# Expert results summed per token in DRAM by accumulating transfers, with tiles of 256 and 128 rows in turn

## The reference

```python
global_idx, weights = _route(tokens, ...)              # two of 8 experts per token, softmax of two scores
h = gelu(einsum('nd,edh->enh', tokens, W1) + b1[:, None, :])      # 256 -> 1024
out_all = einsum('enh,ehd->end', h, W2) + b2[:, None, :]          # 1024 -> 256
out = sum(weights[..., None] * out_all[global_idx, arange(N)[:, None]], axis=1)
x = x + gb * out                                       # gb: one vector per batch
```

## Time and profile before

| what | us |
|---|---|
| median of 3 runs | 3407.97 (3407.96 to 3409.85) |
| the profiled execution's own time, its span | 3422.0 |
| TensorE busy in it | 2651.8 |
| VectorE, ScalarE, GpSimd busy | 1756.1, 1196.3, 565.7 |

### The profile page before, as it was taken

The page is one execution under the profiler, slowest core; times in us unless marked ns, Lnnn a source line. Parts: engine busy times, 40 slices in busy tenths (PEclk is TensorE's granted clock), DMA queues, the critical chain, the costliest instruction groups (busy, mean ns, idle before and its releaser), DMA issues.

```text
span 3422.0 us, 77336 instructions
## 1 busy us (share of the span) xinstructions
PE 2651.8 (77%) x33792; PEld 1955.7 (57%) x33792; DVE 1756.1 (51%) x3803; ACT 1196.3 (35%) x2340; POOL 565.7 (17%) x613
## 2 busy tenths in 40 slices
PE   3468778978896987788788968887696669999980
PEld 3344456556545754564565456555545458888870
DVE  4544766395658547664956585476448310000005
ACT  0322453254336324532543264245226212222210
POOL 0004200600250052006001500430000000000006
PEclk8568986888797889869886988898697789999995
DMA  2122201401120122013011201220110055655545
GB/s 80 31 63 56 51 10 49 99 8 45 51 62 9 45 68 51 8 51 96 11 45 45 68 8 45 69 45 2 57 50 2 18 187 195 195 194 194 194 159 169
DMA packets 229985, 247.00 MB, mean 72 GB/s; under 512 B 147408, under 2 KB 187216, under 8 KB 227344
## 3 DMA queue, kind: packets, MB, share of 16 engines
q1 hardware_dynamic: 223504, 225.27, 21.8%
q0 software_dynamic: 6144, 16.79, 1.5%
HBM read 195.88 MB, written 46.14 MB: 71 GB/s over the span
## 4 chain that ended last, share of the span: by engine, by line
PE 65%; DVE 16%; ACT 9%; issue 5%; POOL 2%; DMA 1%; SPq 1%; POOLq 0%; DVEq 0%; ACTq 0%
PE banks L1944 19%; PE banks L2468 8%; PE banks L2487 8%; PE banks L2259 4%; PE banks L2176 3%; PE banks L2279 2%; PE banks L2284 2%; PE banks L1954 2%; PE banks L2211 2%; POOL arena L1884 2%; DVE hT L1525 2%; PE banks L2046 1%; PE banks L2018 1%; PE banks L2087 1%; ACT arena L895 1%
## 5 line engine op out<-in xcount | busy, mean ns | idle before, releaser
L1944 PE MATMUL banks<-hT,ring 128*128 128x512 f32 x640 | 300.1, 626 | 7.8 <-DVE arena L1377 7.8
L1861 POOL DMA_INDIRECT h_d<-h_tok,pos_now x64 | 65.8, 1028 | 1423.0 <-DVE pos_now L1700 1265.6
L2259 PE MATMUL banks<-arena 32*32 32x64 f32 (+2 forms) x6144 | 187.4, 297 | 140.1 <-DVE arena L1533 64.0
L1082 ACT ACTIVATE arena<-banks,arena 128x256 f32<-128x256 f32 x312 | 130.7, 470 | 457.6 <-PE banks L2468 457.6
L2468 PE MATMUL banks<-arena 128*128 128x256 f32 x1248 | 277.5, 381 | 0.0
L2487 PE MATMUL banks<-arena 128*128 128x256 f32 x1248 | 275.7, 379 | 0.0
L2259 PEld LDWEIGHTS banks<-arena 32*32 32x32 f32 (+2 forms) x6144 | 167.1, 177 | 178.2 <-issue 91.2
L2468 PEld LDWEIGHTS banks<-arena 128*128 128x128 f32 x1248 | 238.4, 191 | 33.1 <-issue 0.4
L2259 PE MATMUL banks<-arena,xn 32*32 32x64 f32 (+2 forms) x6144 | 166.2, 287 | 111.5 <-DVE xn L1533 62.0
L2487 PEld LDWEIGHTS banks<-arena 128*128 128x128 f32 x1248 | 234.2, 190 | 30.3
L1944 PE MATMUL banks<-arena,ring 128*128 128x512 f32 x512 | 224.0, 595 | 6.2 <-ACT arena L852 6.2
(11 more groups left out here) (350 smaller groups left out, 4845.2 us busy)
## 6 DMA issues: line engine op xcount, KB each, us to landing
arena<-in_w_ring SPq DMA_DIRECT2D x78, 1024.0 KB, 5.0
ring<-in_w_ring SPq DMA_DIRECT2D x104, 512.0 KB, 4.5
arena<-h_d SPq DMA_DIRECT2D x39, 256.0 KB, 5.3
y_d<-arena SPq DMA_DIRECT2D x39, 256.0 KB, 5.8
n_d<-NA SPq DMA_DIRECT2D x8, 1024.0 KB, 3.8
arena<-n_d SPq DMA_DIRECT2D x16, 512.0 KB, 5.7
u_d<-arena SPq DMA_DIRECT2D x8, 1024.0 KB, 3.8
NA<-u_d SPq DMA_DIRECT2D x32, 256.0 KB, 5.7
```

The costliest lines, as they stand in the source:

```text
L1082: ins_ = act.activation(hid1[:, i % 2, t], bank[pair][:, half * T1:(half + 1) * T1], ACT.Gelu, bias=b1[:, i % 2, t:t + 1])
L1944: i_ = mm(dst, w[:, k, cols_], rhs(src, k), start=(k == 0), stop=(k == n - 1))
L2259: i_ = mm(bank[4 * hg + h][keys, b * width:(b + 1) * width], K2[rows_, r, b, keys], q, start=(r == 0), stop=(r == 1), skip_group_check=True)
```

## The change

`h_d` gets rows of 516 numbers instead of 256: the token's row, its gate, its number, the two shares and its second expert. Scatters carry all of it. So every tile knows its tokens. VectorE, after the bias, multiplies each row with share and gate, and GpSimd adds it by an accumulating indirect transfer, one for 128 rows, onto the token's residual, which now lies in DRAM in token order (`acc_d`, was `x_d`). Each tile's sums wait until those of the tile before have landed. There is no `y_d`, no gather and no mixing. After the first 42 tiles (`DIRECT`) SP copies `acc_d` to the output, and the last four tiles are added onto the output itself.

Tiles are 25 of 256 rows and 21 of 128, in turn (256, 128, 256, ...), the last four of 256. A tile of 128 rows has half the columns in the first matrix and one block in the second. There are four row buffers.

SP's order changes: when tile `i-1` is scaled, rows of `i+3`, second weights of `i+1`; then, when the gelu of `i` is done, first weights of `i+2`. Ahead of the stage: both weights and rows of tile 0, then the zero writes, then both weights and rows of tile 1.

The plan no longer waits for the other engines' last segment: GpSimd gives its signal (`started`) ahead of its last scatters, and VectorE has no wait there. The shares are computed ahead of the scatters' row numbers. The gate of the second layer's expert block lives in `h_tok`, and what used `h_tok` as scratch uses the gate's old place. The selection matrix of the first layer's routed experts has fewer rows (4 instead of 16 a block).

```diff
+FULLS = -(-(2 * B * L - E1 * (T1 - 1)) // T1)
+HALVES = (2 * B * L + E1 * (P - 1)) // P - 2 * FULLS
+TILES1 = FULLS + HALVES
+SEQ = [n // 2 if n % 2 == 0 else FULLS + n // 2 for n in range(2 * HALVES)] + list(range(HALVES, FULLS))
+SPAN = [2 if slot < FULLS else 1 for slot in SEQ]
+DIRECT = 2 * HALVES
+ROWBUF = 4
...
 # SP
             def load_rows(i):
+                r = sp.value_load(plan_i[0:1, 1, SEQ[i]:SEQ[i] + 1], min_val=0, max_val=E1 * REGION)
+                n = SPAN[i]
+                sp.dma_start(h_rows[:, i % ROWBUF, 0:n], h_d[bass.ds(r, n * P)].rearrange("(j p) d -> p j d", p=P))\
+                    .then_inc(*up16(rows_in[i % ROWBUF]))
+
+            sp.wait_ge(started.handle, 4 * TURNS + 4)
+            sp.wait_ge(plan_ok.handle, 1)
+            load_w1(0)
+            load_w2(0)
             sp.wait_ge(h_out.handle, h_out.base(NSEG))
+            load_rows(0)
+            for e in range(E1):
+                r = sp.value_load(pad_i[0:1, e:e + 1], min_val=0, max_val=E1 * REGION - P)
+                sp.dma_start(h_d[bass.ds(r, P)], zeros).then_inc(*up16(zero_out))
+            sp.dma_start(h_d[E1 * REGION:E1 * REGION + P], zeros).then_inc(*up16(zero_out))
+            load_w1(1)
+            load_w2(1)
             sp.wait_ge(zero_out.handle, 16 * (E1 + 1))
+            for i in range(1, ROWBUF - 1):
                 load_rows(i)
             for i in range(TILES1):
+                if i == 0:
+                    load_rows(ROWBUF - 1)
+                else:
+                    sp.wait_ge(y_ok.handle, i)
+                    if i + ROWBUF - 1 < TILES1:
+                        load_rows(i + ROWBUF - 1)
+                    if i + 1 < TILES1 and i >= 1:
+                        load_w2(i + 1)
+                if i == DIRECT:
+                    sp.wait_ge(y_out[0].handle, 16 * sum(SPAN[0:DIRECT:2]))
+                    sp.wait_ge(y_out[1].handle, 16 * sum(SPAN[1:DIRECT:2]))
+                    sp.wait_ge(x_out.handle, x_out.base(NSEG))
+                    sp.dma_start(out_rows, acc_d[0:B * L]).then_inc(out_ready.handle, 16)
                 if i + 2 < TILES1:
-                    sp.wait_ge(turned.handle, i + 1)
-                    load_rows(i + 2)
                     sp.wait_ge(hid1_ok.handle, 4 * (i + 1))
                     load_w1(i + 2)
-                if i:
-                    sp.wait_ge(y_ok.handle, i)
-                    if i + 1 < TILES1:
-                        load_w2(i + 1)
-                    store_rows(i - 1)
...
 # VectorE, at a segment's end
+                    dve.tensor_copy(h_tok[:, :, SECOND], rs[:, 3])
+                    dve.tensor_scalar(h_tok[:, :, TOKEN].bitcast(I32), token_no[:, :], float(SEG * seg), None, ALU.add)
...
-            dve.wait_ge(started.handle, 4 * (NSEG - PRE) + 4)
             plan_step(dve.memset(zeros, 0.0))
...
 # VectorE, each tile
+                n = SPAN[i]
+                extra = h_rows[:, i % ROWBUF, 0:n]
+                if i >= 2:
+                    dve.wait_ge(y_out[i % 2].handle, 16 * sum(SPAN[i % 2:i:2]))
+                dve.tensor_copy(row_at[:, i % 2, 0:n], extra[:, :, TOKEN].bitcast(I32))
+                plan_step(dve.scalar_tensor_tensor(share[:, i % 2, 0:n], extra[:, :, SECOND], match[:, SEQ[i]:SEQ[i] + 1],
+                                                   extra[:, :, SHARE_GAP], ALU.is_equal, ALU.mult))
+                plan_step(dve.tensor_tensor(share[:, i % 2, 0:n], share[:, i % 2, 0:n], extra[:, :, SHARE_A], ALU.add))
                 dve.wait_ge(down_mm.handle, i + 1)
+                plan_step(dve.tensor_tensor(y_rows[:, i % 2, 0:n], ... b2 ..., ALU.add))
+                for j in range(n):
+                    ins_ = dve.scalar_tensor_tensor(y_rows[:, i % 2, j], y_rows[:, i % 2, j], share[:, i % 2, j:j + 1],
+                                                    extra[:, j, D:2 * D], ALU.mult, ALU.mult)
+                ins_.then_inc(*up(y_ok))
...
 # GpSimd
+            def add_rows(i):
+                target = acc_d if i < DIRECT else out_rows
+                for j in range(SPAN[i]):
+                    spot = bass.IndirectOffsetOnAxis(ap=row_at[:, i % 2, j:j + 1], axis=0)
+                    pool.indirect_dma_start(out=target, out_offset=spot, in_=y_rows[:, i % 2, j], in_offset=None,
+                                            compute_op=ALU.add).then_inc(*up16(y_out[i % 2]))
+
+            pool.wait_ge(x_out.handle, x_out.base(NSEG))
+            for i in range(TILES1):
+                pool.wait_ge(y_ok.handle, i + 1)
+                if i:
+                    pool.wait_ge(y_out[(i - 1) % 2].handle, 16 * sum(SPAN[(i - 1) % 2:i:2]))
+                if i == DIRECT:
+                    pool.wait_ge(out_ready.handle, 16)
+                add_rows(i)
```

More of the change, by code:

```diff
@@ L326, in build @@
         y_rows, o = carve(o, [P, 2, 2, D])
[L327 to L334, removed]
+        zeros, o = carve(o, [P, HW])
+        row_at, o = carve(o, [P, 2, 2])
+        share, o = carve(o, [P, 2, 2])
+        match, o = carve(o, [P, TILES1])
+        num, o = carve(o, [P, 4, TILES1])
+        done_, o = carve(o, [P, TILES1, E1])
+        units, o = carve(o, [P, UNITS])
+        over, o = carve(o, [P, E1, UNITS - 1])
+        upto, o = carve(o, [P, 2, E1, E1])
+        per, o = carve(o, [P, 12, E1])
+        row_at = row_at.bitcast(U32)
         banks_ = ctx.enter_context(nc.psum_tensor("banks", [P, 8, 512], F32))
@@ L1727, in plan_step @@
                 dve.wait_ge(dve_step.handle, dve_step.base(NSEG) + planned[0])
-            dve.wait_ge(started.handle, 4 * (NSEG - PRE) + 4)
             plan_step(dve.memset(zeros, 0.0))
-            nums = plan[:, 0].rearrange("p (a i) -> p a i", i=TILES1)
-            count, tiles, end = plan[:, 1, 0:E1], plan[:, 1, E1:2 * E1], plan[:, 1, 2 * E1:3 * E1]
-            wide = plan[:, 2]
-            expert, first, dummy, local, safe, h_row = [nums[:, a] for a in range(6)]
-            shift, jump = plan[:, 1, 3 * E1:4 * E1], plan[:, 1, 4 * E1:5 * E1]
@@ L1742, in _ @@
-            ends = plan[:, 5, 0:E1 * E1].rearrange("p (e f) -> p e f", e=E1)
-            plan_step(dve.tensor_tensor(ends, tile_no[:, 0:E1].unsqueeze(1).to_broadcast([P, E1, E1]),
-                                        tile_no[:, 0:E1].unsqueeze(2).to_broadcast([P, E1, E1]), ALU.is_le))
-            plan_step(dve.tensor_tensor(upto, ends,
-                                        tiles.unsqueeze(1).to_broadcast([P, E1, E1]), ALU.mult))
-            plan_step(dve.tensor_reduce(end, upto, AX.X, ALU.add))
@@ L1760, in _ @@
-            plan_step(dve.tensor_copy(plan_i[0:1, 0], safe[0:1]))
+            plan_step(dve.tensor_scalar(zeros[:, TOKEN:TOKEN + 1].bitcast(I32), token_no[:, 0:1], float(B * L), None, ALU.add))
+            plan_step(dve.tensor_scalar(units, tile_no[:, :], float(P), None, ALU.mult))
+            count, full_end, kept_end, less, half_end, halves = [per[:, i] for i in range(6)]
+            both, both_end = per[:, 6:8], per[:, 8:10]
+            jump = per[:, 10:12]
+            expert, row_, h_row = num[:, 0], num[:, 1], num[:, 2]
@@ new lines, in _ @@
+            plan_step(dve.tensor_tensor(count, next_row[:, :], region[:, :], ALU.subtract))
+            plan_step(dve.tensor_tensor(over, count.unsqueeze(2).to_broadcast([P, E1, UNITS - 1]),
+                                        units[:, 0:UNITS - 1].unsqueeze(1).to_broadcast([P, E1, UNITS - 1]), ALU.is_gt))
+            plan_step(dve.tensor_reduce(both[:, 1], over, AX.X, ALU.add))
+            n_full = (UNITS - 1) // 2
+            over_f = over[:, :, 0:n_full]
+            plan_step(dve.tensor_tensor(over_f, count.unsqueeze(2).to_broadcast([P, E1, n_full]),
+                                        units[:, 2:UNITS:2].unsqueeze(1).to_broadcast([P, E1, n_full]), ALU.is_ge))
@@ new lines, in _ @@
+            plan_step(dve.tensor_copy(plan_i[0:1, 0], num[0:1, 3]))
+            plan_step(dve.tensor_scalar(jump[:, 0], less, float(T1), float(REGION), ALU.mult, ALU.add))
+            plan_step(dve.scalar_tensor_tensor(jump[:, 1], halves, -float(P), jump[:, 0], ALU.mult, ALU.add))
+            plan_step(dve.scalar_tensor_tensor(jump[:, 1, 0:E1 - 1], less[:, 1:], -float(T1), jump[:, 1, 0:E1 - 1], ALU.mult, ALU.add))
+            for which, (first, last_, ends) in enumerate(parts):
+                n = last_ - first
+                plan_step(dve.tensor_tensor(done_[:, first:last_], done_[:, first:last_],
+                                            jump[:, which].unsqueeze(1).to_broadcast([P, n, E1]), ALU.mult))
@@ L1768, in _ @@
[L1768 to L1773 removed]
+            plan_step(dve.tensor_scalar(match, expert, -1.0, float(E1), ALU.mult, ALU.add))
@@ L1855, in turn @@
                     settle()
+                    if not nxt:
+                        pool.sem_inc(started.handle, 1)
                     pool.wait_ge(*at(h_tok_ok, 2))
@@ L2484, in _ @@
                     pe.wait_ge(y_ok.handle, i - 1)
-                for j in range(2):
```

(1 more changed line is left out.)

238 lines of the change are left out of this document (93 added, 145 removed).

## The result

The changed kernel takes **3433.84 us** (median of 4 runs, 3432.6 to 3436.21) where the kernel before takes 3407.97: ratio 1.0076, 95% interval 1.0063 to 1.0089. It is slower by 26 us, 0.8%; 74 us less had been forecast. The profiled execution has a span of 3431.6 us and spends 662 us between the first matrix product of the last stage (2757.50) and the end of the last one (3420.00), where the kernel before spends 557 and the forecast had 575 (508 + 59 + 8).

A forecast was written before the change was run, and what follows sets the result against it. TensorE was taken to bound the last stage, with stretches without it before and after. Terms -91 - 4 - 48 + 59 + 8 + 2 = -74 us gave span 3348, scaled to 3334 us; range 3285 to 3390.

The forecast's parts named there:

- The loads: Last stage: half tiles' first weights land late, TensorE stalls 2.8 us in each of 21 pairs, +59 us.
- E: The end of a full tile's second matrix; first weights expected at E + 13.4, needed at E + 10.6.
- The forecast's pessimistic end: Loads in the last stage: slower loads, rows and sums give E + 15.3, 26.1 us a pair, +98 us.
- Rival (2): Last stage: TensorE's clock falls in each stall, +32 us; chance 0.15.
- The half tiles' matrices: Last stage: fewer rows, a half tile's first matrix 3.5 us, TensorE's work 508 us, -48 us.
- The copy: At tile 42: the 4.2 MB copy stands ahead of tile 44's first weights, +8 us.
- The tail: After the last matmul: gathers, mixing and stores go, 97.7 us becomes 6.3, -91 us.
- The start: Ahead of the last stage: matmuls start near 2762.8 instead of 2767.2, held by tile 1's rows, -4 us.
- The sums: A full tile's two accumulating transfers beside the loads: 0.8 us each with the target's read, 1.3 together.
- Rival (3): GpSimd's sums, each waiting for the one before, set the pace from a landing time of 11.3 us; chance 0.06.
- The scaling: Whole kernel: run median is 0.9959 of the profiled span, taken as profiling's cost, turning 3348 us into 3334.
- The chance for slower, 0.06: Whole kernel: chance given to a time above the kernel before, beside 0.91 for faster and 0.03 for same.

The follow-up runs named there:

- the clock held up: Changed kernel with 16 unit-matrix products on TensorE ahead of each wait for a half tile's first weights: 3398.58 us, ratio 0.9969.
- the run without stalls: Changed kernel with the first weights issued ahead of the wait for the tile before, and so ahead of the copy: 3285.85 us, ratio 0.9638.
- the run with the other order: Changed kernel with TensorE doing tile 0's first matrix before turning tile 1 at the stage's start: 3424.8 us, ratio 1.0042.
- the order in the queue (two runs): Changed kernel with first weights ahead of the wait for the tile before, 3285.85 us; or behind it but ahead of rows and second weights, 3302.37 us.

## Why the prediction was wrong, point by point

The mechanism was the forecast one: the landing of the half tiles' first weights ends the wait, at 20 of the 21 half tiles and at tile 43. Its size was not. Against the forecast's stage of 575 us the trace has 662.5, 87.5 more; the tail has 5.3 more.

- **The loads: the step that failed first.** Forecast: first weights at E + 13.4, pair 24.25. Measured: E + 15.1 in the mean, and 26.2 a pair with the clock held up. By the windows of the pair that is shown (E + 14.75): 3.45 us to the first packet (3.5 forecast); the rows 2.35 (1.5): I gave them the 351 GB/s of a flow of large packets, and they went at 209; what the sums take for themselves 0.60, the rest of them lying beside the loads (1.3); second weights and bias row 3.85 (4.0); first weights 3.9 until the end of their last packet (3.0); bias columns and hand-over 0.6 (0.1). The rate that I took from the middle of a flow tells when nine in ten packets have started (E + 13.3 in the mean), not the last (E + 14.2), and from there to TensorE's start it is another 0.8. Why the rows came at 209 GB/s no run tells. The forecast's pessimistic end, E + 15.3 and 26.1 a pair, came close in its sum, by other terms; I had taken a value near the middle because each term had a row, though the rows were of means. That is 1.95 us a pair, some 40 us.
- **The clock: a rival that was no alternative.** Rival (2), priced +32 with a chance of 0.15, came true at every one of the 22 waits, on top of the stall, and costs 36 us by the run, 38 by the busy time. The two stalls of the earlier trace rows had been read as a coin's two sides; but the forecast's own stall of 2.8 us was about as long as the one of 2.9 after which the clock fell, and every us by which the loads came later made it longer. The Trainium skill, page "TensorE: Matmul & The Clock Gate", section "HAM oscillation — how this bites in real kernels", tells of loops in which each wait for a transfer brings the lower clock anew; the trace agrees, with 0.51 after a wait of 4.15 us and 1.00 where 0.8 was left of it. A stall and its clock belong in one term. Pairs together: 28.2 - 24.25, 79 us over the 20 pairs timed.
- **The half tiles' matrices.** Right: the first matrix takes 3.57 us in the run without stalls (3.5 forecast), and the stage 511.7 there (508 forecast). The -48 was there to be had, and the order of the loads took it and more.
- **The copy.** +8 forecast, 13.6 measured by the ratios, 12.2 by the traces. The copy waits for sums, and these landed 8.35 and 9.16 us after their issue ended; I had counted the landing at 3.3 and let the queue decide.
- **The tail.** 6.3 forecast, 11.6 measured: the issues are 1.56 us, not 0.97 with 0.3 between; the last packet ends 7.3 us after the last matmul (3427.34), and the span ends 4.3 us behind that, where it ended 0.8 us after the last packet in the kernel before (3421.17 of 3422.0).
- **The start.** From the last products of the router to the first matrix -4 forecast, -2.2 measured (42.3 us before, 40.1 after). That tile 1's rows and not tile 0's decide was right, as the run with the other order shows.
- **The sums.** Rival (3) did not come. A transfer of 128 rows takes 7.3 us (median) from issue to landing, under the 11.3 from which it decides, and the run with early weights has them all at 21.5 us a pair. Its packets are 128 of 1 KB and some 108 ns, 0.87 us of all 16 engines, as the forecast's 0.8; a plain write goes in 32 packets of 159 ns, 0.32. The Trainium skill's factor of two (page "Collectives: The Full Stack", section "The bandwidth ceiling: the fold count and why AG ≠ RS ≠ AR") is stated there of the reducing step of a ring between cores. Here the packets' time is 2.7 times that of the plain write. The accumulating packets are also smaller, 1 KB against 4; which part of the 2.7 is due to that no run tells. In the time it is 1 us a pair.
- **The scaling.** The 0.9959 that I took for what profiling adds was a long execution of the segments; it subtracted the right 14 us for another reason.

The chance for slower, 0.06, was put on one mechanism only. The terms above add up: forecast 3334, loads 40, clock 38, tail 5, copy 6, start 2 give 3425; the remaining 9 are the first matrices of the stage, partly at the lower clock (13.36 us to the start of the first second matrix, where 10.9 would do at full clock), pairs somewhat longer than these two terms (83 us in 21 pairs, where they give 78), and the spread of the segments. What is shown is the order in the queue (two runs), the clock (one run) and the copy; that a single DMA engine finishes last is read from packet times and not tried.

## What to carry to other kernels

When work per tile shrinks, every load gets a due time that moves up, and the queue's order must follow: put the load that is wanted first at the head, and measure the due time against the landing of the last packet of a chain of loads, not against a rate. A stall that the forecast itself expects has its clock price in the same term, since both come from the same late load (idle stretches of 0.8 and 2.5 us left the clock up here, 2.9 and 4.15 brought it down, and between 3.0 and 3.4 us, with plain writes, both came about). An order that costs nothing in one kernel (1.0011 here with 256 rows, shorter rows and no sums) can cost 133 us in another.

## What the hardware showed that was not expected

- The load of the first weights ends in a trail: the last tenth of its 256 packets of 4096 bytes took 0.9 us in the mean (0.4 to 1.9), as long as the some 80 in front of them.
- An accumulating transfer of 128 rows takes GpSimd 1558 ns to issue where a plain one takes 966, and moves in packets of 1 KB where the plain one moves in packets of 4 KB.
- The changed kernel and its eight variants whose last transfers are accumulating ones of GpSimd ended 4.3 us after their last packet, the one with plain writes of GpSimd 6.7 us after it; the three kernels whose last transfer is a store of SP ended 0.8 us after it.
